# Moving the copy of v and the normalisation from VectorE to ScalarE, with v's bias folded into later biases, in a three-layer transformer decoder

## The reference, cut to what matters

```
# layer 0: causal self attention
q, k, v = split(x @ W_qkv + b_qkv)
x = layernorm(x + softmax(causal(q k^T / 4)) v @ W_proj + b_proj)
# layer 1: cross attention to ctx (k and v from ctx), masked by a [128,128] mask
x = layernorm(x + softmax(mask((x wq^T + bq)(ctx wk^T + bk)^T / 4)) (ctx wv^T + bv) @ wo^T + bo)
# layer 2: attention without a projection, beside 8 experts of which 2 count for a token
q, k, v = split(x @ W_qkv + b_qkv)
gate = softmax(x @ W_gate + b_gate); top 2 of 8 -> combine
x = layernorm(x + softmax(q k^T / 4) v + sum_e combine_e (x @ W_e + b_e))
# layernorm(x) = (x - mean) / sqrt(var + 1e-5), per token over 256 features
```

## Time and profile before

| | us |
|---|---|
| median of 3 runs | 971.46 |
| lowest, highest | 968.36, 973.17 |
| profiled execution, its own time | 970.37 |
| its span from the first to the last instruction | 968.7 |

### The profile page before, as it was taken

One profiled execution on the slowest core, in us unless ns is written; L12 is line 12 of the kernel. 1 busy time (PEld: TensorE's weight loads), 2 busy tenths in 40 slices (PEclk: granted clock), 3 DMA queues, 4 the chain that ended last, 5 costly groups with the idle time before them and its releaser, 6 DMA issues.

```text
span 968.7 us, 28521 instructions
## 1 busy us (share of the span) xinstructions
PE 885.6 (91%) x9964; PEld 743.2 (77%) x9964; DVE 862.8 (89%) x3931; ACT 530.4 (55%) x1083; POOL 409.7 (42%) x490
## 2 busy tenths in 40 slices
PE   5798999998889999999999999999999999999986
PEld 3787888787878888888887777777778777777774
DVE  4799999999889999989898789998888888888985
ACT  4576767666657676767676444444344434444422
POOL 5678878786664444444444222211222122212200
PEclk8999999999999999999999999999999999999999
DMA  5565555554434534343433222222222222222210
GB/s 176 159 176 165 139 157 155 163 163 131 130 83 129 148 105 129 106 128 106 128 96 106 68 67 77 63 69 71 78 73 62 66 67 79 78 78 78 61 29 23
DMA packets 98161, 100.87 MB, mean 104 GB/s; under 512 B 10700, under 2 KB 90596, under 8 KB 98020
## 3 DMA queue, kind: packets, MB, share of 16 engines
q1 hardware_dynamic: 98020, 99.05, 36.8%
HBM read 18.53 MB, written 4.19 MB: 23 GB/s over the span
## 4 chain that ended last, share of the span: by engine, by line
DVE 43%; PE 35%; issue 9%; ACT 5%; DMA 4%; POOL 2%; SPq 1%; DVEq 0%; POOLq 0%; ACTq 0%
PE work L477 15%; DVE x_all L999 7%; DVE max_scores L918 6%; PE work L607 6%; DVE neg_max L921 6%; PE max_scores L562 4%; PE scores L586 4%; PE work L616 3%; DVE neg_max L918 2%; DVE combine_first L901 2%; ACT attn L767 2%; DVE z L942 2%; DVE x_all L973 2%; DVE bn_stats L955 2%; DVE x_all L1011 1%
## 5 line engine op out<-in xcount | busy, mean ns | idle before, releaser
L918 DVE CUSTOM_DVE_ANT_0 max_scores<-max_scores,mask_qk 128x128 f32<-128x128 f32 x1024 | 260.6, 324 | 16.9 <-PE max_scores L562 16.1
L767 ACT ACTIVATE attn<-scores 128x512 f32<-128x512 f32 x384 | 215.2, 597 | 105.8 <-PE scores L586 101.0
L562 PE MATMUL max_scores<-k_stack,q_stack 126*128 126x128 bf16 x1536 | 148.7, 222 | 12.2 <-DVE neg_max L918 8.7
L586 PE MATMUL scores<-q_stack,k_stack 128*128 128x128 bf16 x1536 | 142.3, 222 | 9.4 <-DMA q_stack<-neg_max_t 4.9
L918 DVE DVE_READ_ACCUMULATOR2_ANT neg_max<- 128x1 f32 x1024 | 142.7, 139 | 0.0
L1038 POOL TENSOR_TENSOR q_full<-q_full,q_parts 128x512 f32<-128x512 f32 x48 | 56.9, 1184 | 183.9 <-ACT q_parts L725 183.9
L562 PEld LDWEIGHTS max_scores<-k_stack,q_stack 126*128 126x128 bf16 x1536 | 99.9, 98 | 45.2 <-issue 18.4
L999 DVE SCALAR_TENSOR_TENSOR x_all<-work,combine,x_all 128x256 f32<-128x256 f32 x256 | 122.6, 479 | 6.9 <-PE work L477 1.6
L477 PE MATMUL work<-split_hi,w_hi 128*128 128x256 f32 x384 | 118.6, 309 | 8.2 <-DVE split_lo L820 8.2
L586 PEld LDWEIGHTS scores<-q_stack,k_stack 128*128 128x128 bf16 x1536 | 97.9, 98 | 33.8 <-ACT attn L767 12.3
L607 PE MATMUL work<-attn,v_ones 128*32 128x128 f32 x3072 | 103.8, 275 | 19.5 <-DVE x_all L999 17.1
(11 more groups left out here) (115 smaller groups left out, 2013.2 us busy)
## 6 DMA issues: line engine op xcount, KB each, us to landing
k_stack<-k_parts SPq DMA_DIRECT2D x288, 128.0 KB, 2.4
q_stack<-q_parts SPq DMA_DIRECT2D x288, 128.0 KB, 2.4
in_t<-in_xt SPq DMA_DIRECT2D x16, 256.0 KB, 3.0
x_all<-in_x SPq DMA_DIRECT2D x16, 256.0 KB, 3.0
in_t<-in_ct SPq DMA_DIRECT2D x16, 256.0 KB, 3.5
out<-x_all SPq DMA_DIRECT2D x16, 256.0 KB, 2.1
stage<-in_e SPq DMA_DIRECT2D x4, 512.0 KB, 5.1
stage<-in_qk SPq DMA_DIRECT2D x2, 512.0 KB, 4.9
```

The costliest lines, as they stand in the source:

```text
L562: mm = pe.matmul(dst[:, b, h2, :], head(QS, n, 2 * p + h2, b, ROWS), head(KS, n, 2 * p + h2, b, ROWS), start=(b + h2 == 0), stop=(b + h2 = ...
L586: mm = pe.matmul(dst[:, b, h2, :], head(KS, n, 2 * p + h2, b, rows), head(QS, n, 2 * p + h2, b, rows), start=(b + h2 == 0), stop=(b + h2 = ...
L767: act.activation(attn("exp", n, p)[:, :, :], SS[g % 2][:, :, :, :].rearrange("k b h q -> k (b h) q"), ACT.Exp).then_inc(probs_done, 1)
L918: ins = dve.tensor_tensor_reduce(scores, scores, MQ[l][:, :], -1.0, HUGE, ALU.add, ALU.min, NM[n % 2][:, b, h:h + 1])
```

## The change

**Layers 0 and 1.** VectorE no longer adds v's bias. ScalarE copies v from PSUM into `v_ones` in one instruction of 128x512 per item (`v_copy`, kind `va`). The bias of v goes through the output projection instead: once per layer, TensorE multiplies it with the projection weights' high and low parts (`output_bias`, kind `bo`: four float32 matmuls with 256 columns), and VectorE adds the result to the row of output biases (`bias_sum`, kind `bor`), for which the first `residual` of the layer waits.

**Layer 2.** VectorE copies v without a bias. v's bias becomes two more rows (high and low part) of the expert bias product, whose combine weights are set to one at the start, so `BIAS_ROWS` goes from 24 to 26.

**All layers.** ScalarE does the normalisation as x * rstd + (-mean * rstd), two instructions of 128x256 per item (`norm`). For the second operand GpSimd gets two more small instructions per item: the negated mean, and its product with rstd, which waits for the power.

**Loads and table.** `row_bias` shrinks from 1288 to 520 columns, `col_bias` grows from 12 to 18. The table of times is new throughout (of it only two rows with kinds added or removed are shown).

```diff
...
-BIAS_ROWS = 3 * E
+BIAS_ROWS = 3 * E + 2
...
-RB_V = [0, 2 * D, 4 * D]
-RB_O = [D, 3 * D]
-RB_COLS = 4 * D + VG
-PERIOD = [16.5, 18.13, 24.96]
+RB_O = [0, D]
+RB_GATE = 2 * D
+RB_COLS = 2 * D + E
+PERIOD = [16.51, 18.09, 25.01]
...
-     "kl": [-27.05], "ks": [-32.63, -30.95, -28.04], "v": [-15.71], "ve": [-15.14],
...
-     "norm": [31.1], "causal": [3.28, 4.07, 5.37, 5.63, 5.86, 9.0, 9.57, 10.4]},
...
+     "kl": [-26.96], "ks": [-39.04, -36.71, -31.39], "v": [-17.46],
...
+     "norm": [31.08], "causal": [3.4, 3.85, 4.83, 5.1, 6.4, 8.76, 9.32, 10.16], "va": [-15.88]},
...
+BIAS_TIMES = [(-14.0, -12.5), (130.0, 132.0)]
...
 ORDER = sorted([(base(n) + t, kind, n, part) for n in range(NITEM)
                 for kind, times in TIMES[layer(n)].items() for part, t in enumerate(times)]
                + [(t, kind, j, 0) for j, times in enumerate(PIECE_TIMES)
-                  for kind, t in zip(("wload", "whi", "wlo"), times)])
+                  for kind, t in zip(("wload", "whi", "wlo"), times)]
+               + [(t, kind, l, 0) for l, times in enumerate(BIAS_TIMES) for kind, t in zip(("bo", "bor"), times)])
 WHEN = {(kind, n, part): t for t, kind, n, part in ORDER}
...
+READER[("bo", 0)] = ("bor", 0)
+def reader(kind, n, part):
+    return ("va", 0) if kind == "v" and layer(n) < 2 else READER[(kind, part)]
...
+        ZERO = sb("zero", [P, PB])
+        NEG = sb("neg_mean", [P, NL, PB])
+        SHIFT = sb("neg_mean_rstd", [P, NL, PB])
...
+            def output_bias(l, part):
+                if l == 0:
+                    pe.wait_ge(first_lo, 2)
+                else:
+                    pe.wait_ge(w_lo_done, PIECES.index("vo1") + 1)
+                dst = mine("bo", l)
+                for c in range(C):
+                    for k, w in enumerate((WH[l], WL[l])):
+                        mm = pe.matmul(dst[:, 0:D], COLB[:, l, 2, c:c + 1].to_broadcast([P, P]),
+                                       w[:, c, 3 * D:4 * D].bitcast(F32), start=(c + k == 0), stop=(c + k == C))
+                mm.then_inc(bo_psum, 1)
...
             def values(n, f):
...
-                if f == 0:
-                    for b in range(PB if l == 2 else 1):
-                        pe.wait_ge(v_done[b], turn(n) if b else n + 1)
+                if f == 0 and l == 2:
+                    for b in range(PB):
+                        pe.wait_ge(v_done[b], turn(n))
+                elif f == 0:
+                    pe.wait_ge(va_done, n + 1)
...
+            def v_copy(n, part):
+                act.wait_ge(v_psum[0], n + 1)
+                if n == 0:
+                    act.wait_ge(setup_p, 1)
+                if n >= VALUES:
+                    act.wait_ge(pv_psum, PV_TURN[(n - VALUES, 1)] + 1)
+                act.activation(VA[n % VALUES][:, :, 0:H * VH].rearrange("p b (h d) -> p b h d", h=H)[:, :, :, 0:DH],
+                               bank("v", n)[:, :].rearrange("p (b h d) -> p b h d", b=PB, h=H), ACT.Copy).then_inc(va_done, 1)
+            def normalise(n, part):
+                l, x = layer(n), pair(n)
+                act.wait_ge(rs_done, n + 1)
+                for b in range(PB):
+                    ins = act.activation(x[:, b, :], x[:, b, :], ACT.Identity, bias=SHIFT[:, l, b:b + 1], scale=RS[:, l, b:b + 1])
+                ins.then_inc(norm_done, 1)
...
             dve.memset(NHALF[:, :], -0.5)
             dve.memset(EPSC[:, :], EPS)
+            dve.memset(ZERO[:, :], 0.0)
             for j in range(2):
-                dve.memset(CB[j][:, :, :], 0.0)
+                setup_link(dve.memset(CB[j][:, :, :], 0.0))
+                dve.memset(CB[j][:, :, 3 * E:BIAS_ROWS], 1.0)
             setup_link(dve.memset(GN[:, :], 0.0))
...
             def v(n, b):
-                l, src, dst = layer(n), bank("v", n, b), VA[n % VALUES]
+                src = bank("v", n, b)
                 dve.wait_ge(v_psum[b], turn(n) if b else n + 1)
-                if n >= VALUES and b == 0:
+                if b == 0:
...
-                if l == 2:
-                    dve.tensor_tensor(GL[:, b, :], src[:, D:VG], RB[:, RB_V[2] + D:RB_V[2] + VG], ALU.add)
-                for j in range(PB):
-                    if l == 2 and j != b:
-                        continue
-                    o = 0 if l == 2 else j * D
-                    ins = dve.tensor_tensor(dst[:, j, 0:H * VH].rearrange("p (h d) -> p h d", h=H)[:, :, 0:DH], src[:, o:o + D].rearrange("p (h d) -> p h d", h=H),
-                                            RB[:, RB_V[l]:RB_V[l] + D].rearrange("p (h d) -> p h d", h=H), ALU.add)
-                ins.then_inc(v_done[b], 1)
-                if l == 2 and b == 1:
+                dve.tensor_tensor(GL[:, b, :], src[:, D:VG], RB[:, RB_GATE:RB_GATE + E], ALU.add)
+                dve.tensor_copy(VA[n % VALUES][:, b, 0:H * VH].rearrange("p (h d) -> p h d", h=H)[:, :, 0:DH],
+                                src[:, 0:D].rearrange("p (h d) -> p h d", h=H)).then_inc(v_done[b], 1)
+                if b == 1:
...
+            def bias_sum(l, part):
+                bias = RB[:, RB_O[l]:RB_O[l] + D]
+                dve.wait_ge(bo_psum, l + 1)
+                dve.tensor_tensor(bias, bank("bo", l)[:, 0:D], bias, ALU.add).then_inc(bo_done, 1)
...
-            def normalise(n, part):
-                l, x = layer(n), pair(n)
-                dve.wait_ge(rs_done, n + 1)
-                for b in range(PB):
-                    ins = dve.tensor_scalar(x[:, b, :], x[:, b, :], MV[:, l, b, 0:1], RS[:, l, b:b + 1],
-                                            ALU.subtract, ALU.mult)
-                ins.then_inc(norm_done, 1)
...
+                if turn(n) == 1:
+                    pool.wait_ge(bo_done, l + 1)
                 for b in range(PB):
...
             def rstd(n, part):
...
-                pool.tensor_tensor(VE[:, l, :], MV[:, l, :, 1], EPSC[:, :], ALU.add).then_inc(ve_done, 1)
+                pool.tensor_tensor(VE[:, l, :], MV[:, l, :, 1], EPSC[:, :], ALU.add)
+                pool.tensor_tensor(NEG[:, l, :], ZERO[:, :], MV[:, l, :, 0], ALU.subtract).then_inc(ve_done, 1)
                 pool.wait_ge(ve_done, n + 1)
-                pool.tensor_tensor(RS[:, l, :], VE[:, l, :], NHALF[:, :], ALU.pow).then_inc(rs_done, 1)
+                pool.tensor_tensor(RS[:, l, :], VE[:, l, :], NHALF[:, :], ALU.pow).then_inc(power_done, 1)
+                pool.wait_ge(power_done, n + 1)
+                pool.tensor_tensor(SHIFT[:, l, :], NEG[:, l, :], RS[:, l, :], ALU.mult).then_inc(rs_done, 1)
...
-    biases = [(a(L0_attn_b_qkv)[:D], a(L0_attn_b_qkv)[D:2 * D]), (a(L0_xattn_bq), a(L0_xattn_bk)),
...
```

57 lines of the change are left out of this document (29 added, 28 removed), and 45 rows, old and new, of the table TIMES.

## The result

The changed kernel takes 926.08 us (median of 4 runs, 922.34 to 927.58) against 971.73 us for the kernel before (4 runs, 968.36 to 973.17). The ratio is 0.9529, with a 95% interval of 0.9491 to 0.9567: faster by 4.7%, 45.7 us. The prediction was 952 us with a range of 938 to 968. Some executions run 1 to 2% longer at a lower granted clock, the profiled one of e12 among them (985.53 us, clock 0.964); all comparisons of times are between the others.

What follows compares the result with a forecast made beforehand. Layer 0 was taken as bound by VectorE, layer 1 by TensorE, layer 2 by a ring of both. 11.2 + 1.5 + 7.0 + 1.7 - 2.0 - 0.8 = 18.6 off 970.4 gave 952 us, range 938 to 968.

Steps and rivals of the forecast that it cites:

- layer 2: Layer 2: normalisation leaves VectorE's part of the chain, 0.5 us an item, 7.0 us in all, between 0 and 9.0.
- Its upper bound: Layer 2: at most 9.0 us gained; the item's 1.84 us over TensorE's work doesn't forbid the whole gain.
- The rule: GpSimd shares SBUF interfaces with VectorE; layer 0's removed pair worth 0.80 instead of 0.86 us, the sum 0.8 us less.
- Layer 0: Layer 0: VectorE falls under TensorE, which reaches 95.5%; 0.86 us an item, 11.2 us, between 0 and 19.9.
- shared ring: Rival: ScalarE, GpSimd and DMA hold layer 0's period, 0.2 us an item gained there; 967.5 us, no change; chance 0.15.
- Layer 1: Layer 1: VectorE loses about 1.6 us an item but TensorE has little idle time; 1.5 us, between 0 and 5.
- ScalarE's added work: Copy of v and normalisation: 1.5 us an item in layers 0 and 1, 0.9 in layer 2; costed at nothing.
- the slower rival: ScalarE's list blocks in order once it reaches the normalisation before GpSimd has finished rstd; 981 us; chance 0.10.
- The start: Before VectorE's setup: shorter `row_bias` saves 2.2 us, small memsets cost 0.4; 1.7 us gained, between 0 and 2.2.
- The bias product: TensorE, layers 0 and 1: 8 records each at 0.29 us, 4.6 us if unhidden, 0 if covered; cost 2.0 us.
- The end: Last normalisation: two more GpSimd steps, a handover and the slower pair cost 0.8 us, between 0.5 and 1.5.

Runs made afterwards that it cites:

- e12: Kernel before with layer 2's normalisation on VectorE placed later, behind the gate's steps, and the item's store later: 971.05 us, ratio 0.9978.
- e4: Kernel before with GpSimd's four subtractions per item of layer 2 cut to 8 columns instead of 256: 939.28 us, ratio 0.9633.
- e1: Kernel before with the new table for layer 2 alone, every engine keeping its work: 950.29 us, ratio 0.9737.
- e2: Changed kernel with the old table for layer 2, normalisation still on ScalarE: 935.16 us, ratio 0.9581.
- e10: Changed kernel with all three old tables, the copy of v taking the time of v's bias: 962.29 us, ratio 0.9889.
- e8: Changed kernel with layer 0's normalisation left out, a one-column ScalarE copy signalling in its place: 922.02 us, ratio 0.9476.
- e7: Changed kernel with the old tables for layers 0 and 1, layer 2's rows staying new: 956.80 us, ratio 0.9827.
- e9: Kernel before with all three new tables, v's bias and the normalisation staying on VectorE: 980.84 us, ratio 1.0078.
- e14: Changed kernel with three extra GpSimd subtractions per item beside layer 2's gate steps, result unread: 940.92 us, ratio 0.9682.
- e5: Changed kernel with layer 0's normalisation back on VectorE at the same place in the table: 949.43 us, ratio 0.9761.
- e13: Kernel before with GpSimd's four subtractions replaced by memsets of about their length from layer 2's fifth item on: 959.32 us, ratio 0.9864.

## Why the prediction was wrong

**The step that failed: layer 2.** I gave it 7.0 us, "between 0 and 9.0", from 0.5 an item, and the measured stretches from item 33 on give 24.1 + 8.9 = 33 us. The prediction said that the normalisation was on the chain for 0.64 us and that the rest of the chain is VectorE's own list. That list I took for work. The waits were read, the durations of the instructions between them were not: 2.4 us an item of it were stalls behind GpSimd, and a stall that is shown as a long instruction is in no view of waits. e4 shows that they alone are worth 2.28 us an item, e1 and e2 that each half of the change ends most of them.

**The new table had no term at all.** The sum prices who does the work and takes the order for neutral. With the old order the engines' change gives 1.1% (e10, ratio 0.9889), with the new one 4.7%. The forecast direction holds for the engines alone too, so it wasn't luck; but the forecast gain of 2% is near neither.

**Its upper bound failed with it.** "The item holds 26.18 - 24.34 = 1.84 us over TensorE's work": TensorE's work is 23.8 us (full windows of e4 and of the kernel after), which leaves 2.4. And 9.0 us was the chain's piece, 0.64 times 14, as if removing a piece could free no more than its length.

**The rule was named and its price put on the wrong lines.** The prediction saw that VectorE's normalisation took between 0.398 and 1.260 us, brought GpSimd's shared interfaces up for it, and priced that at 0.06 us an item of layer 0. In layer 0 the largest that went away was another one, `split_lo`, before and after,

```profile
L820 DVE TENSOR_TENSOR split_lo<-in_t,split_hi x10: 694/1637/1649, 89.0 to 227.0; 128x512 fp32r<-128x512 f32 x10
```

```profile
L868 DVE TENSOR_TENSOR split_lo<-in_t,split_hi x11: 737/744/986, 74.8 to 228.4; 128x512 fp32r<-128x512 f32 x11
```

whose stall was 0.76 us an item before and is 0.12 after.

**Layer 0: too large.** I took 11.2 us; items 1 to 12 give 3.7, 0.34 an item instead of 0.86. VectorE did come down (89% of the window; I had said 91%), but TensorE stayed at 90.6% and not at 95.5%. What was late next is the ring in which ScalarE, the DMAs and TensorE wait for one another in turn; waits of 75 to 255 us after:

```profile
PE scores L616 <- DMA q_stack<-neg_max_t: 9.1, 11, 1.8
```

In the earlier trace rows the largest of TensorE's waits there named VectorE's maxima; the largest now is for the DMA that brings q's stacked rows. The rival "shared ring" had this mechanism (0.2 us an item in layer 0), and its mark, a period above 15.5, was missed narrowly at 15.36. e8 shows the moved pair itself in that ring with 0.40 us. And e7 shows that a lighter VectorE alone doesn't shorten layer 0: with the old order it makes it slower, 16.68 us.

**Layer 1: right in kind.** 0.33 us an item, some 5 us where I took 1.5 and allowed 0 to 5. e7 gives 16.63 for the engines alone and e9 16.68 for the order alone. With both, TensorE is full there as well, 174.58 of 174.64 us; the window from item 17 to item 28 of the kernel after:

```profile
323.50:498.14 174.64, 174.58 (x2223) 150.28 (x2221) 148.41 (x914) 135.50 (x276) 83.95 (x111) 1.00 0.44 120
```

**ScalarE's added work: hidden, at another size.** The pair took 1.09 us, where I took 0.9 (and allowed up to 1.3):

```profile
L821 ACT ACTIVATE x_all<-x_all,neg_mean_rstd,rstd 128x256 f32<-128x256 f32 x96 | 52.3, 598 | 6.4 <-POOL neg_mean_rstd L1121 6.4
```

The Trainium skill's formula (ScalarE: Activation LUTs, What ACT_TABLE_LOAD costs) had given 1.08; the rows that I preferred read PSUM. Its wait for GpSimd is 6.4 us in all, 4.69 of them at the end: the slower rival's condition was never met.

**The start: 1.0 us, not 1.7.** I took 1.7 us from the shorter constants. The setup starts at 10.25 instead of 10.17, and its wait is as long, 3.11 us. But the load of `in_vo` ahead of both, whose size didn't change, also landed later in that execution, by 1.3 us, as ScalarE's wait for it shows (before, after), and then the setup:

```profile
7.86 1.06 ACT L676 ACTIVATE w_hi<-k_stack 128x1024 fp32r<-128x1024 f32 x1 [1.96 <-DMA k_stack<-in_vo]
...
9.13 1.06 ACT L708 ACTIVATE w_hi<-k_stack 128x1024 fp32r<-128x1024 f32 x1 [3.33 <-DMA k_stack<-in_vo]
...
10.25 0.17 DVE L878 TENSOR_SCALAR q_bias_scaled<-col_bias 128x6 f32<-128x6 f32 x1 [3.11 <-DMA expert_bias<-in_eb]
```

From there to the setup it is 2.31 us before and 1.12 after. Over all profiles it is 2.12 to 2.31 us in the seven kernels with the old loads and 1.10 to 1.27 in the nine with the new ones, while that landing itself varies from 7.69 to 9.68 us in both. So the shorter constants are worth 1.0 us where I took 1.7, and one pair of profiles hides it. Item 1's statistics come 2.6 us later in this pair. The six profiles with the old layer 0 have them at 75.5 to 77.9 us, the three with the new one unchanged (after, e2, e14) at 77.1 to 78.1, so most of the 2.6 us is the spread of the former; what is left isn't explained. **The bias product** cost TensorE 3.9 us of busy time, 0.38 us a record where I took 0.29. The second one, in layer 0, is on the chain that ended last; the first isn't:

```profile
159.21 1.78 PE work L511 x8
```

**The end** was right: from the last statistics to the end of the last pair 966.03 - 963.18 = 2.85 before and 3.63 after, 0.8 more, as forecast. The last pair:

```profile
922.08 1.09 ACT L821 ACTIVATE x_all<-x_all,neg_mean_rstd,rstd 128x256 f32<-128x256 f32 x2 [4.69 <-POOL neg_mean_rstd L1121]
```

## What to carry to other kernels

Ask for shortest, median and longest duration of every short VectorE form before summing up its list: a median several times the shortest, ending together with a GpSimd instruction, is a wait that no view of waits shows, and it can be worth more than all the work that one would move. A form that is always held up has no short one in its own kernel, so look for it in another, and where held-up instructions overlap, go by busy time. Expect then that moving anything, work or order, changes what falls beside GpSimd, for better (e1, e2), for worse (e5, e9) or to no effect (e12), and try both halves together before judging either. Don't take share times period for TensorE's floor in a stage where it has gaps. And before comparing the start of two profiles, see how much it varies from one execution to the next.

## What the runs showed of the hardware

Which VectorE instructions GpSimd holds up. Counted in layer 2: instructions that began at least 0.05 us after a GpSimd instruction and would by their usual duration have ended over 0.1 us before it did, and how many of them were longer than usual by over 0.1 us.

| VectorE's form | sources | beside a subtraction | beside a memset (e13) |
|---|---|---|---|
| TENSOR_SCALAR, gate steps | SBUF | 13 of 13 (e14), 1 of 1 (before) | 30 of 30 |
| CAST `neg_max_parts`, `gate_index_f` | SBUF | 15 of 15 (before) | 14 of 14 |
| TENSOR_TENSOR `combine` | two in SBUF | 13 of 13 (before), 13 of 13 (e14) | none fell there |
| TENSOR_TENSOR `x_all` with `z` | two in SBUF | 7 of 7 (before) | 0 of 8 |
| TENSOR_TENSOR `z`, SCALAR_TENSOR_TENSOR `x_all` | PSUM and SBUF | 0 of 25 (before), 0 of 28 (after) | 0 of 30 |
| CAST `combine_t` | PSUM | 0 of 14 (after) | none fell there |
| TENSOR_REDUCE `neg_max` | SBUF | 0 of 14 (after) | none fell there |
| MAX8, MATCH_VALUE_LOAD, FIND_INDEX8, gate steps | SBUF | 0 of 78 (e14) | none fell there |
| RECIPROCAL `gate_recip` | SBUF | 0 of 13 (e14) | none fell there |

Instructions that begin within 0.05 us of GpSimd's go either way: `combine_first` was held up at 721.92, 0.01 us ahead of the subtraction, while `combine_hi` at 723.92, 0.02 us behind the next one's start, passed. The Trainium skill (SBUF — State Buffer, Who interferes with whom) says that the pair of ports which the two engines share goes whole to the one that comes first, until its instruction ends; that copies, casts and tensor_scalar can take it in their 2-port modes; that two inputs in SBUF contend with a GpSimd instruction that reads, not with one that only writes; and that tensor_reduce never does. The rows of these forms agree, the line with 7 of 7 and 0 of 8 with the clause on writing. What the runs add is the price: the rest of GpSimd's instruction, up to 1.0 us for ones of 0.17 to 0.29; and the four instructions that wait behind a memset together and then end together (e13).

The granted clock of TensorE fell with its gaps in layer 0: 0.99 at 163.11 us busy of 180 (after) and 0.89 at 149.94 (e9).
